# Row maxima of the attention scores from six part products in 48 rows, two maps at a time in the two row halves of TensorE's array, with normalisation on VectorE and one step less in the combination

## What is computed

```
q = rope(xn @ Wq)   # 4 x 1024 x 32 heads of 8
k = rope(xn @ Wk)   # 16 heads of 8
v = xn @ Wv         # 8 heads of 16
attn1 = softmax(causal(q1 k1^T * scale)) @ v
attn2 = softmax(causal(q2 k2^T * scale)) @ v
attn  = attn1 - lambda_full * attn2
```

## Time and profile before

| what | us |
|---|---|
| median of 3 runs | 2068.59 (2059.54 to 2070.35) |
| the profiled execution, its time | 2063.18 |
| its span, first to last instruction | 2061.4 |
| chunk loop and first maxima | to about 173 |
| attention units, from the last maxima of unit 0 to those of unit 31 | 173.1 to 1171.2 |
| mean granted TensorE clock | 0.958 |
| PE busy over the span | 1895.9 (92%) |
| DVE busy over the span | 1456.4 (71%) |

### The profile page before, as it was taken

How to read it: one execution, slowest core, us unless ns; L and a number is a source line. 1 busy time by engine, 2 the same in 40 slices (tenths; PEclk the granted TensorE clock), 3 DMA queues, 4 the chain that set the end, 5 groups by cost and what they waited for, 6 DMA issues and landing times. The chain is left out here.

```text
span 2061.4 us, 42263 instructions
## 1 busy us (share of the span) xinstructions
PE 1895.9 (92%) x11851; PEld 1123.2 (54%) x11851; DVE 1456.4 (71%) x3497; ACT 1061.3 (51%) x2554; POOL 709.6 (34%) x753
## 2 busy tenths in 40 slices
PE   6878999999999999999999989999899999999954
PEld 4543434444343344443443347777788887878843
DVE  6778888899888898898898724444478764333354
ACT  3323666666676666666666634444333322444432
POOL 5762532111112223232232205777414331333323
PEclk8876999999999999999999989999999999999986
DMA  4433432212223122121121112433213122222386
GB/s 109 134 111 87 140 116 76 67 26 69 64 55 86 40 58 59 39 63 49 48 63 41 34 30 87 123 119 123 98 65 108 60 88 90 86 90 87 103 269 208
DMA packets 204889, 178.83 MB, mean 87 GB/s; under 512 B 92360, under 2 KB 184824, under 8 KB 204408
## 3 DMA queue, kind: packets, MB, share of 16 engines
q1 hardware_dynamic: 185736, 128.34, 22.0%
q0 software_dynamic: 15888, 46.16, 6.4%
q10 hardware_dynamic: 3168, 3.15, 0.5%
HBM read 108.36 MB, written 76.90 MB: 90 GB/s over the span
## 5 line engine op out<-in xcount | busy, mean ns | idle before, releaser
L1779 DVE TENSOR_REDUCE mx<-ps 128x1 f32<-128x512 f32 (+3 forms) x1536 | 760.7, 548 | 88.7 <-PE ps L891 67.7
L1346 ACT ACTIVATE fbuf<-ps 128x512 f32<-128x512 f32 (+3 forms) x1024 | 459.3, 508 | 238.8 <-PE ps L902 230.8
L887 PE MATMUL ps<-rbuf 72*128 72x512 bf16 (+3 forms) x1536 | 504.0, 336 | 26.0 <-DVE mx L1779 12.4
L902 PE MATMUL ps<-rbuf 75*128 75x512 bf16 (+3 forms) x1536 | 500.4, 333 | 20.3 <-DMA rbuf<-mrows 19.1
L902 PEld LDWEIGHTS ps<-rbuf 75*128 75x128 bf16 x1536 | 149.7, 98 | 330.5 <-ACT fbuf L1346 143.2
L1346 ACT ACTIVATE gbuf<-ps 128x512 f32<-128x512 f32 (+2 forms) x512 | 211.0, 470 | 90.6 <-PE ps L902 89.6
L738 POOL TENSOR_SCALAR_AFFINE_SELECT gbuf<-gbuf 128x512 f32<-128x512 f32 x96 | 62.1, 647 | 514.4 <-ACT gbuf L1346 514.4
L745 POOL DMA_INDIRECT y_scr<-wstage,bidx x138 | 139.1, 1008 | 280.0 <-ACT wstage L1412 260.5
L887 PEld LDWEIGHTS ps<-rbuf 72*128 72x128 bf16 x1536 | 151.2, 98 | 153.8 <-DVE mx L1779 122.4
L917 PE MATMUL ps<-fbuf 128*32 128x512 f32 (+3 forms) x2048 | 229.7, 521 | 2.3 <-issue 0.2
L891 PE MATMUL ps<-maskq,identb 128*128 128x128 bf16 x1024 | 228.8, 224 | 0.0
(11 more groups left out here) (269 smaller groups left out, 3039.4 us busy)
## 6 DMA issues: line engine op xcount, KB each, us to landing
rbuf<-q_scr SPq DMA_DIRECT2D x192, 96.0 KB
gbuf<-y_scr SPq DMA_DIRECT2D x16, 1024.0 KB, 6.1
xs_scr<-in_pad SPq DMA_DIRECT2D x8, 1360.0 KB, 6.1
gbuf<-xs_scr SPq DMA_DIRECT2D x69, 136.0 KB, 2.1
gbuf<-xe_scr SPq DMA_DIRECT2D x69, 136.0 KB, 2.1
rbuf<-k_scr SPq DMA_DIRECT2D x192, 48.0 KB
q_scr<-gbuf SPq DMA_DIRECT2D x48, 128.0 KB
a_scr<-fbuf SPq DMA_DIRECT2D x64, 64.0 KB, 2.2
```

The lines of the kernel that those rows point to most:

```text
L887: ins = pe.matmul(o, qst[par][0:PROWS, i // 4, m, P * (i % 4):P * (i % 4 + 1)], kst[par][0:PROWS, m % 2, 512 * piece:512 * piece + width], ...
L902: pe.matmul(o, kst[par][0:SROWS, m % 2, P * j:P * (j + 1)], qst[par][0:SROWS, h, m, t0:C], start=True, stop=True).then_inc(b_scores, 1)
L1346: act.activation(prob(s)[:, t0:C], ps[:, s % SRING, t0:C], ACT.Exp, scale=SCALE).then_inc(b_exp, 1)
L1779: dve.tensor_reduce(mx[:, i // 4, piece, n:n + 1], ps[:, SRING + s % SRING, 0:width], AX, ALU.max, negate=True).then_inc(b_maxed, 1)
```

## The change

Seven edits stand in it.

1. The maxima are taken from six of the nine part products (those whose part numbers add up to less than three), in 48 rows instead of 72. Two maps are done by two matmuls of 48 rows, one on partitions 0 to 47, one on 64 to 111 (`max_pair`, `L917` of the changed kernel), into two banks of the ring; then come the two masks. The score matmuls are as before.
2. `max_pair` is called at odd steps, LEAD is 42, and it waits until only one of the three banks may be unread.
3. The 48 rows lie in buffers of their own. `load_max` fills them with 24 transfers a unit (12 for q of 24, 16 or 8 partitions x 1024, 12 for k of 8 x 1024), ahead of `load_qk`. For the first unit this lies ahead of the stores of chunk 2. `scores` now waits for `load_qk` itself.
4. `normed` runs on VectorE for all chunks, behind the first two rests of a chunk; `stats` moves behind the third product.
5. ScalarE issues the load of x for a chunk behind the copy of a transposed chunk, one step earlier than before (`fetch`).
6. `combine` takes the factor of the second map into its last operation; one VectorE operation of 128 x 8 goes.
7. B_STEPS, a count for a semaphore, goes with it from 20 to 16.

```diff
-LEAD = 43
+LEAD = 42
...
+            def load_max(u, par, first=False):
+
+                qm, km = (qm0, km0) if first else (qmt[par], kmt[par])
+                for x in range(2):
+                    at = MTILE * x
+                    for b in range(PARTS):
+                        rows = slice(at, at + HD * (PARTS - b))
+                        for y in range(2):
+                            sp.dma_start(qm[y][rows], q_scr[0:PARTS - b, :, u, 2 * y + x, :].rearrange("a d t -> (a d) t")
+                                         ).then_inc(b_m_in[par], 16)
+                        for r in range(PARTS - b):
+                            sp.dma_start(km[at + HD * r:at + HD * (r + 1)], k_scr[:, b, u, x, :]
+                                         ).then_inc(b_m_in[par], 16)
+                        at += HD * (PARTS - b)
...
             def unit(u, par, first, last):
                 if not last:
+                    if not first:
+                        sp.wait_ge(b_maxed, JOBS * u)
+                    load_max(u + 1, 1 - par)
                     load_qk(u + 1, 1 - par, None if first else u)
...
-                if not (first and s < SRING):
-                    pe.wait_ge(b_maxed, JOBS * u + s + 1 - SRING)
+                if not (first and s + 1 < SRING):
+                    pe.wait_ge(b_maxed, JOBS * u + s + 2 - SRING)
                 width = min(512, P * (i + 1) - 512 * piece)
...
+                for x in range(2):
+                    rows = slice(MTILE * x, MTILE * x + MROWS)
+                    ins = pe.matmul(ps[:, MX + (s + x) % SRING, 0:width], qm[m0 // 2][rows, P * i:P * (i + 1)],
+                                    km[rows, 512 * piece:512 * piece + width], start=True, stop=not diag)
...
-                    if s < JOBS - LEAD:
-                        max_matmul(u, par, s + LEAD)
-                    elif not last:
-                        max_matmul(u + 1, 1 - par, s + LEAD - JOBS)
+                    if s % 2 == 1 and s < JOBS - LEAD:
+                        max_pair(u, par, s - 1 + LEAD, first)
+                    elif s % 2 == 1 and not last:
+                        max_pair(u + 1, 1 - par, s - 1 + LEAD - JOBS)
...
-                if c + 2 < NCH:
-                    normed(c + 2, c % 2)
...
                 if c + 2 < NCH:
-                    dve.wait_ge(a_sd, c + 3)
-                    dve.reciprocal(rst[:, h], rst[:, h]).then_inc(a_rstd, 1)
+                    normed(c + 2, h)
...
-                r2v = rec[:, :].rearrange("p (n c) -> p n c", c=2)[:, :, 1]
-                go(dve.tensor_scalar(r2v, r2v, lamneg, None, ALU.mult))
```

More of the change, by code:

```diff
@@ L43 @@
 ONES_FROM = 64
+MROWS = sum(HD * n for n in range(1, PARTS + 1))
+MTILE = 64
 GROUPS = [(h, j) for h in range(2) for j in range(4 * (h + 1))]
@@ L185, in build, with spare @@
         assert len(probs) * MAPS == PRING and JOBS % PRING == 0
+        qmt, kmt = [], []
+        for x in range(2):
+            at = MAPS * C + 3 * T // 2 * x
+            q, k = carve(gbuf[:, at:at + 3 * T // 2].bitcast(BF16), [(2, T), (T,)])
+            qmt.append((q[:, 0], q[:, 1]))
+            kmt.append(k)
+        def spare(w, k):
+            return w[:, k, NE - 1].bitcast(BF16)
+        qm0, km0 = (spare(WZH, 0), spare(WZH, 1)), spare(WZL, 0)
         def prob(s):
@@ L262, in build @@
         b_v_in = [sem(f"b_v_in{p}") for p in range(2)]
+        b_m_in = [sem(f"b_m_in{p}") for p in range(2)]
         b_shift_in = [[sem(f"b_shift_in{p}{h}") for h in range(2)] for p in range(2)]
@@ L874, in _, with max_pair @@
             ST, MX, OT = 0, SRING, 6
-            def max_matmul(u, par, s, first=False):
-                i, piece, m = MAXJ[s]
+            def max_pair(u, par, s, first=False):
+                qm, km = (qm0, km0) if first else (qmt[par], kmt[par])
+                i, piece, m0 = MAXJ[s]
                 if s == 0:
-                    pe.wait_ge(b_qk_in[par][0], 96 * (u // 2 + 1))
-                if s == MAXA:
-                    pe.wait_ge(b_qk_in[par][1], 96 * (u // 2 + 1))
-                if not (first and s < SRING):
-                    pe.wait_ge(b_maxed, JOBS * u + s + 1 - SRING)
+                    pe.wait_ge(b_m_in[par], 16 * MLOADS * (u // 2 + 1))
+                if not (first and s + 1 < SRING):
+                    pe.wait_ge(b_maxed, JOBS * u + s + 2 - SRING)
                 width = min(512, P * (i + 1) - 512 * piece)
-                o = ps[:, MX + s % SRING, 0:width]
                 diag = piece == i // 4
-                ins = pe.matmul(o, qst[par][0:PROWS, i // 4, m, P * (i % 4):P * (i % 4 + 1)],
-                                kst[par][0:PROWS, m % 2, 512 * piece:512 * piece + width],
-                                start=True, stop=not diag)
+                for x in range(2):
+                    rows = slice(MTILE * x, MTILE * x + MROWS)
+                    ins = pe.matmul(ps[:, MX + (s + x) % SRING, 0:width], qm[m0 // 2][rows, P * i:P * (i + 1)],
+                                    km[rows, 512 * piece:512 * piece + width], start=True, stop=not diag)
+                    if not diag:
+                        ins.then_inc(b_maxs, 1)
                 if diag:
-                    ins = pe.matmul(o[:, width - P:width], identb[:, :], maskq[:, :], start=False, stop=True)
-                ins.then_inc(b_maxs, 1)
+                    for x in range(2):
+                        pe.matmul(ps[:, MX + (s + x) % SRING, width - P:width], identb[:, :], maskq[:, :],
+                                  start=False, stop=True).then_inc(b_maxs, 1)
             def scores(u, par, s, first):
@@ L1303, in a_step @@
                 high_part(c, h, 1)
-                if ahead > 0:
+                if c + 1 < NCH:
                     copy_turned(c + 1, 1 - h)
-                if ahead > 1:
+                if c + 3 < NCH:
+                    fetch(c + 3)
+                if c + 2 < NCH:
                     deviation(c + 2)
@@ L1319, in _ @@
             act.activation(lame, lams, ACT.Exp).then_inc(act_consts, 1)
-            a_step(1, 1)
-            for b in range(1, B - 1):
-                a_step(2 * b, 0)
-                a_step(2 * b + 1, 1)
-            a_step(NCH - 2, 0, 1)
-            a_step(NCH - 1, 1, 0)
+            for c in range(1, NCH):
+                a_step(c, c % 2)
             act.wait_ge(a_split, 3 * NCH)
```

30 lines of the change are left out of this document (14 added, 16 removed).

## The result

| | us |
|---|---|
| before, median of 4 runs | 2065.7 (2059.54 to 2070.35) |
| after, median of 4 runs | 2531.48 (2524.98 to 2539.19) |
| ratio | 1.226, interval 1.221 to 1.231 |
| profiled execution of after, its span | 2523.2, granted clock 0.827 |
| forecast | 2444, range 2290 to 2575 |

What follows compares the result with a forecast made beforehand. TensorE was tightest, VectorE close behind, but SyncE's transfer chain would decide: 30 units x 12.6 us = 378, other terms -2.5, on 2063.2 gives 2438.7 us; the profiled execution stands 5.4 below the median, so 2444 us, range 2290 to 2575.

Steps and rivals of the forecast that it cites:

- What bounds, and the place of the delay: In each attention unit, SyncE's new transfers make the shift of half 1 late for TensorE: 10.9 us more, 92%.
- 24 transfers at 0.53 us, 12.7 us: On SyncE, ahead of the twelve loads: issue time of the new transfers, 12.7 us a unit, bounds 8.7 to 16.6.
- The chain from step 33 to 16, 31.0 us: From TensorE's step 33 through SyncE's transfers and loads to the next unit's step 16: 31.0 us, before 20.05.
- The clock, 1.7 us a unit, at most 3.4: TensorE's lower granted clock after idling for transfers: 1.7 us a unit lost, between 0 and 3.4.
- Step 7 and step 16 wait in turn: TensorE idles twice a unit: around 6 us for the new transfers, then 3 to 6 us for half 1's shift.
- The pair, 0 in the sum: TensorE's side-by-side maxima: 4.0 us a unit saved, 5.5 us paid for array switches; 0 put into the sum.
- The wait for two banks, 0, at most 1 us: TensorE waits for VectorE before each pair of maxima: at most 1 us a unit on the chain, taken as 0.
- VectorE's removed step, 0: In the combination, one VectorE operation less: 0.75 us a unit, all inside the delay, so 0.
- Chunk loop -10, first pairs +2: Ahead of the units: normalisations on VectorE +10.6 us, earlier x load up to -27, taken as -10; first pairs +2 us.
- Unit 0, +5.5: In the first unit the shift of half 1 moves too: about half of 10.9 us, so 5.5 us more.
- SyncE absorbing the transfers: Rival: SyncE's spare 1.5 us hides the transfers, under 0.06 us each, and array switches decide: 2120 us, chance 3%.
- The faster case: Rival: halves without a switch, SyncE hiding the transfers, VectorE becoming the bound: 93 us less, 1966 us with chunk loop, 4%.

Runs made afterwards that it cites:

- a kernel without the delay: Changed kernel with its 24 transfers moved into SyncE's idle time and maxima on the whole array: pairs waiting for two banks 2169.75 us, single maxima 2055.85 us.

## Why the prediction was right, and where it was short

**What bounds, and the place of the delay: right.** The shift of half 1 is late behind 24 transfers, 22.5 us behind the shift of half 0 (928.98 - 906.48), before 14.1. The trace of after and the run with moved loads agree.

**24 transfers at 0.53 us, 12.7 us: too high by 2.1.** They took 919.24 - 908.61 = 10.6 us, 0.44 each, inside the bounds. They are issued faster than the k loads they were taken from, the last one of a group in 0.28 us.

**The chain from step 33 to 16, 31.0 us: right but for that term.** 28.9 on average, and 28.4 in the unit shown: 4.86 to the first transfer (forecast 5.15), 10.6 (12.7), 9.2 for the twelve loads (9.0), 0.5, 3.2 from the shift to step 16 (3.42).

**The clock, 1.7 us a unit, at most 3.4: right in kind, far too small.** From step 16 to 33, where the forecast had 11.7 + 1.7 us, after needs 18.4 on average (20.05 in the unit shown). The same instructions at 0.99 take 12.6, so the low clock costs 5.8 us a unit, outside both ends of the term. The size came from the one case in the earlier trace rows, where 2.46 us of idling were followed by 3.7 us at 0.54. The runs show that the low stretch is longer when idling comes in every unit: between 300 and 1100 us about 7 us a unit with 12 transfers and 13 with 24, both over before step 16, and 22 us a unit in after, where it reaches behind step 16. After has both a second wait and the half-array pairs, and no run separates the two; which of them keeps the clock low for so long stays open. I carried a duration from a single case over to a repeated one.

**Step 7 and step 16 wait in turn: right,** 29 and 28 times, with 2.0 and 3.2 us on average. For step 7 some 6 us were said, which was too much: the maxima ahead of it are late by then too.

**The pair, 0 in the sum: right for a 512-column pair, and for the reason given.** 0.21 us for the two changes against a stream of 0.22; the halves are worth 1 us of 2170.

**The wait for two banks, 0, at most 1 us: wrong, but mostly hidden here.** 1.5 us a unit, and the order of pairs, which has no term of its own, 2.0 more; together (2169.75 - 2055.85) = 114 us on a kernel without the delay. The estimate assumed that VectorE would catch up in front of step 16, and didn't ask what two maxima at once do to a ring of three banks in all the steps between. In the changed kernel most of it lies inside SyncE's delay, as the forecast said of the terms ahead of step 16: only 12.62 - 11.69 = 0.9 us falls between step 16 and 33.

**How the unit adds up.** By the table after takes 15.6 us a unit more than before: 8.8 from step 33 to 16, the transfers less the slack and the small gains in the other terms, and 6.7 from step 16 to 33, 5.8 of it the clock and 0.9 the pairs. The forecast had 10.9, 1.7 and 0. Its marks were to stand 43 to 44 us apart instead of 31.7, though its own sum gives 31.7 + 12.6 = 44.3, and the mean distance before is 32.2.

**VectorE's removed step, 0: right.** Ratio 1.000 on the kernel before.

**Chunk loop -10, first pairs +2: the signs of the two parts right, their sum wrong.** The first mark moved by +0.9, where -8 was said. Its parts follow from three first marks: 156.6 us with the chunk loop and the combination (16.5 earlier than before), 167.3 with the 24 first transfers too (10.7 back), 174.0 in after and 172.7 with the loads in the idle time (5.4 to 6.7 back for the pairs). VectorE's wait for x fell by 22 us, from 27.0 to 4.8; its normalisations, at 0.74 us each instead of 0.443 and 32 instead of 8, cost it 18.6 us more. That leaves 3.6 of the 16.5 us; where the rest comes from wasn't traced. What I put at nothing are the first 24 transfers, since SyncE has idle time later; they stand on the path there and cost 10.7 us. **Unit 0, +5.5:** its distance to the next mark is 47.0 us (221.0 - 174.0) instead of 45.6, so 1.4.

**The rivals.** SyncE absorbing the transfers needed 0.06 us each; 0.44 were measured. The faster case needed halves without a switch, which 0.21 us excludes. The time landed above the forecast because the clock (+4.1 us a unit) and the pairs (+0.9) outweighed the transfers (-2.1). That it still fell into the range is in part luck: the clock lay outside its own ends, and the transfers made up for half of that.

**A version that is a little faster than both** came out of the study: the chunk loop with the combination alone, 2048.51 us, 0.7% faster than before (0.5 to 0.9%). Of the change it keeps what has nothing to do with pairs.

## What to carry to other kernels

Before adding transfers to a queue, look at what stands behind them on that queue and when it is needed: the same 24 transfers a unit cost 313 us or nothing, by their place alone. When a size is taken from an event that happened once, ask whether it holds when the event comes in every turn. These matmuls ran side by side only where both output banks were free at one time, so with a ring of three a pair trades a saved stream for a wait on the engine that empties it. And a kernel that gets slower by some per cent in code that nobody touched may be waiting for instructions behind a loop's branch: look for idle time that ends in "issue", and shift the code before looking for a cause in the edit.

## What the hardware showed that I hadn't expected

- The granted clock stayed at 0.51 for 20.05 us while TensorE was busy for 20.05 us, behind two idlings of 4.56 and 2.81 us whose ends lie 11.5 us apart. Over 300 to 1100 us the time at the lower level was 379 us in after, 249 us with 24 transfers, 152 us with 12, 3 us before.
- A change between full-array matmuls and row halves cost about 0.1 us in each direction (0.54 instead of 0.43 us on the way in, 0.32 instead of 0.22 on the way out, at a clock near 1).
- Thirty-two small instructions ahead of a loop took 103 us off a kernel of 2158 us (2157.67 to 2054.92).
- Transfers of 24 x 1024 or 8 x 1024 were issued by SyncE every 0.44 us, the twelve q and k loads every 0.75 us (9.0 us for twelve).
